# A recurrence's read-out on TensorE: one product per channel, or four channels as four 32-column tiles

## The reference

```python
r, k, v, w = ...                      # each (b, l, 32 heads, 8)
g = silu(xg @ Wg.T)
def step(s, rkvw):                    # s: (b, head, i, j), 8 x 8 per head
    a   = k_t[..., :, None] * v_t[..., None, :]
    out = einsum('bhi,bhij->bhj', r_t, u * a + s)
    s   = a + w_t[..., :, None] * s
    return s, out
# per head of 8 outputs: subtract the mean, divide by the deviation
og = normalized(out) * gn_w + gn_b
x1 = x + og * g @ Wo.T                # then the feed-forward part
```

## Time and profile before

| what | value |
|---|---|
| median of three executions | 2283.3 us (2282.72 to 2286.55) |
| span of the profiled execution, first to last instruction | 2282.6 us |
| its own time beside the span | not recorded; the median stands 0.7 us above the span |
| mean granted TensorE clock | 0.950 |
| TensorE busy | 1881.2 us, 82% |
| VectorE busy | 1497.5 us, 66% |
| ScalarE busy | 883.1 us, 39% |
| GpSimd busy | 879.3 us, 39% |

### The profile page before, as it was taken

How to read it: one execution, slowest core, us unless ns; L and a number is a source line. 1 busy time by engine, 2 the same in 40 slices (tenths; PEclk the granted TensorE clock), 3 DMA queues, 4 the chain that set the end, 5 groups by cost and what they waited for, 6 DMA issues and landing times. The chain is left out here.

```text
span 2282.6 us, 31354 instructions
## 1 busy us (share of the span) xinstructions
PE 1881.2 (82%) x10673; PEld 1165.9 (51%) x10673; DVE 1497.5 (66%) x2416; ACT 883.1 (39%) x1696; POOL 879.3 (39%) x928
## 2 busy tenths in 40 slices
PE   3888887889878897888978889788887899788765
PEld 2565444654447544564446644465445654356423
DVE  4654579736886369764697547973589746876274
ACT  1434442534425334254333543244432543425202
POOL 4522256312762137421373215631256313752060
PEclk9999999999999999999999999999998999999967
DMA  5000011010210102000020101201011010200030
GB/s 152 1 1 22 6 34 43 1 37 1 47 29 1 37 1 61 15 27 11 15 61 1 31 8 29 47 1 32 7 42 34 1 36 1 61 15 10 2 75 9
DMA packets 69291, 59.79 MB, mean 26 GB/s; under 512 B 34664, under 2 KB 52216, under 8 KB 69112
## 3 DMA queue, kind: packets, MB, share of 16 engines
q1 hardware_dynamic: 49592, 41.70, 8.2%
q10 hardware_dynamic: 18976, 15.80, 2.3%
q0 software_dynamic: 544, 0.03, 0.0%
HBM read 19.23 MB, written 4.19 MB: 10 GB/s over the span
## 5 line engine op out<-in xcount | busy, mean ns | idle before, releaser
L1498 POOL TENSOR_TENSOR soft_ring<-soft_ring,seg_max 128x512 f32<-128x512 f32 x256 | 326.9, 1277 | 586.1 <-DVE seg_max L1337 585.5
L1044 ACT ACTIVATE soft_ring<-soft_ring 128x512 f32<-128x512 f32 x256 | 161.1, 629 | 580.6 <-POOL soft_ring L1498 577.4
L1460 POOL TENSOR_TENSOR late<-late 128x520 f32<-128x520 f32 x128 | 212.4, 1659 | 64.4 <-DMA late<-late 49.7
L1331 DVE SCALAR_TENSOR_TENSOR soft_ring<-bank,mask 128x512 f32<-128x512 f32 x256 | 174.7, 683 | 94.7 <-PE bank L839 44.4
L660 PE MATMUL bank<-late,pick 128*128 128x512 f32 x256 | 162.2, 721 | 76.9 <-DVE late L1185 76.9
L583 PE MATMUL bank<-early 128*128 128x512 f32 x384 | 201.9, 611 | 18.4 <-ACTq L1037 13.6
L1173 DVE TENSOR_TENSOR_SCAN late<-late 128x520 f32<-128x520 f32 x128 | 204.2, 1595 | 18.3 <-POOL late L1462 11.0
L1337 DVE TENSOR_REDUCE seg_max<-soft_ring 128x8 f32<-128x512 f32 (+1 forms) x256 | 174.9, 683 | 26.8 <-DVE early L1352 9.5
L846 PEld LDWEIGHTS bank<-ident,soft_ring 128*128 128x128 f32 x1024 | 130.3, 148 | 80.5 <-issue 69.1
L839 PEld LDWEIGHTS bank<-early,qring 128*128 128x128 f32 x1024 | 138.4, 203 | 64.4 <-issue 61.7
L846 PE MATMUL bank<-ident,soft_ring 128*128 128x128 f32 x1024 | 164.0, 285 | 0.5 <-ACT soft_ring L1044 0.2
(11 more groups left out here) (242 smaller groups left out, 3456.1 us busy)
## 6 DMA issues: line engine op xcount, KB each, us to landing
late<-late SPq DMA_DIRECT2D x128, 260.0 KB, 3.0
c<-in_ctx ACTq DMA_DIRECT2D x8, 512.0 KB, 3.8
x<-in_x ACTq DMA_DIRECT2D x8, 512.0 KB, 6.5
out_x<-late SPq DMA_DIRECT2D x8, 512.0 KB, 6.4
w<-in_L_xattn_mlp_w ACTq DMA_DIRECT2D x2, 1024.0 KB
mask<-in_mask_BxS_ik SPq DMA_DIRECT2D x8, 256.0 KB, 3.7
mask<-in_mask_Bx1xSxS_ff ACTq DMA_DIRECT2D x8, 128.0 KB, 3.8
wkv<-in_L_xattn_kv_w ACTq DMA_DIRECT2D x1, 512.0 KB
```

The lines of the kernel that those rows point to most:

```text
L1044: af(soft[:, u % SOFT, :], soft[:, u % SOFT, :], ACT.Exp).then_inc(sig("exp"), 1)
L1331: stt(out=cuts(u, soft[:, u % SOFT, :]), in0=cuts(u, t[:, :]), scalar=HD1 ** -0.5 if u < UNITS else 1.0 / HD2, in1=mask.unsqueeze(1).broad ...
L1460: tt(aj[:, n % 2, :], kP[:, k, :, :].rearrange("p b t -> p (b t)"), vj[:, n % 3, :], ALU.mult).then_inc(sig("kv_done"), 1)
L1498: tt(s, s, seg_max[:, u % SOFT, 0:segs].unsqueeze(2).broadcast_to([128, segs, 512 // segs]), ALU.subtract).then_inc(sig("sub"), 1)
```

## The change

Output channels are collected four at a time. The `rs` ring has four buffers. In every fourth scan stage TensorE issues four products, each with a stationary of 128 x 32 columns, into PSUM partitions 0 to 31, 32 to 63, 64 to 95 and 96 to 127. Column 16*e + head of the stationary sums that head for the channels 4*e to 4*e + 3 (e = 0, 1); the two collections of a half accumulate. So head outputs come out ordered by channel: partition 32*(j % 4) + 16*(j // 4) + head. What meets them has to be in that order too: the rows of Wv and Wg, the columns of Wo, the head scales gn_w and gn_b, the matrices for centering, variance and bonus. They are permuted once in the setup: VectorE copies the rows and Wo in the new order before TensorE transposes them, and Wv and Wg on the way out of PSUM. The read of `vj` is now from 16 adjacent partitions. GpSimd's memset of `pick`, whose line is not in the diff, covers the new, smaller tensor (64 elements a partition instead of 1024).

```diff
+RS = 4
-        pick = sb("pick", [128, HS, 128])
+        pick = sb("pick", [128, 2, 2, 16])
-        rs = cut(late, 8808, 2, 512)
+        rs = cut(late, 8808, RS, 512)
+        def by_lane(ap):
+            return ap.rearrange("p (h e c) -> p c e h", e=2, c=4)
+        def lane(j):
+            return 32 * (j % 4) + 16 * (j // 4)
@@ setup, TensorE
-                nc.tensor.transpose(t[:, 0:128], vrows, ident[:, :]).then_inc(full, 1)
+                nc.tensor.transpose(t[:, 0:128], vrows, ident[:, :])
+                pe.wait_ge(sig("lane_rows"), 1)
+                nc.tensor.transpose(t[:, 128:256], vrows_by_lane, ident[:, :]).then_inc(full, 1)
+                    if w == "Wo":
+                        pe.wait_ge(sig("lane_wo"), 1)
+                        src = wo_by_lane
@@ setup, VectorE
-                for j in range(HS):
-                    nc.vector.tensor_copy(pick[:, j, :].rearrange("p (h j) -> p h j", j=HS)[:, :, j], block8[:, :, j])
+                (heads8, same8, pick and center8 built from block8 and ident: a memset, five copies, a reduction, the old center8 operation)
+                dve.wait_ge(sig("rows_all"), 1)
+                dve.wait_ge(sig("more_rows_in"), 16 * (15 + 2))
+                nc.vector.tensor_copy(vrows_by_lane.rearrange("p (c e h) -> p c e h", c=4, e=2), by_lane(vrows)).then_inc(sig("lane_rows"), 1)
+                dve.wait_ge(sig("square_in"), 16 * len(SQUARE))
+                for o in range(KT):
+                    for m in range(KT):
+                        at = slice(128 * m, 128 * m + 128)
+                        ins = nc.vector.tensor_copy(wo_by_lane[:, o, at].rearrange("p (c e h) -> p c e h", c=4, e=2),
+                                                    by_lane(cut(early, 512 * SQUARE.index("Wo"), KT, E)[:, o, at]))
+                ins.then_inc(sig("lane_wo"), 1)
                 normalize_ahead(dve, link)
...
+                    if w in ("Wv", "Wg"):
+                        (four copies of 128 x 128 through by_lane instead of one of 128 x 512)
@@ SyncE
-                            sp.dma_start(vj[:, n % 3, :], vP[j::HS, k, :, :]...
+                            sp.dma_start(vj[:, n % 3, :], vP[lane(j):lane(j) + 16, k, :, :]...
@@ TensorE, scan stages
-                            if 0 <= n < KT * HS:
+                            if 0 <= n < KT * HS and n % 4 == 3:
                                 pe.wait_ge(sig("rs_ready"), n + 1)
-                                mm(t[:, :], pick[:, j, :], rs[:, j % 2, :], start=j == 0, stop=j == HS - 1).then_inc(
-                                    full if j == HS - 1 else sig("rs_used"), 1)
+                                for c in range(4):
+                                    ins = mm(t[32 * c:32 * c + 32, :], pick[:, e, :, :], rs[:, (n - 3 + c) % RS, :], start=e == 0, stop=e == 1)
+                                ins.then_inc(full if e == 1 else sig("rs_used"), 1)
@@ VectorE, read(n)
-                            if n >= 2:
-                                m = n - 2
-                                if m % HS == HS - 1:
-                                    filled(("o3", m // HS))
+                            if n >= RS:
+                                quad = (n - RS) // 4
+                                if quad % 2 == 1:
+                                    filled(("o3", quad // 2))
                                 else:
-                                    dve.wait_ge(sig("rs_used"), m - m // HS + 1)
+                                    dve.wait_ge(sig("rs_used"), quad // 2 + 1)
```

More of the change, by code:

```diff
@@ L167, in build @@
         nmax0 = sb("nmax0", [128, 2 * NP, 2])
-        late = sb("late", [128, 10856])
+        late = sb("late", [128, 9832 + 512 * RS])
         x3 = sb("x3", [128, NP, E])
@@ L195, in build @@
         vrows = early[:, 8192:8320]
+        vrows_by_lane = early[:, 8320:8448]
+        wo_by_lane = cut(early, 8448, KT, E)
         soft = soft_ring[:, :, :]
@@ L445, in _ @@
                 nc.vector.tensor_copy(ones2[:, 0:16], half[:, :, :].rearrange("p a b -> p (a b)"))
-                link(nc.vector.scalar_tensor_tensor(out=center8[:, :], in0=flat8, scalar=-1.0 / HS, in1=ident[:, :], op0=ALU.mult, op1=ALU.add))
-                for j in range(HS):
-                    nc.vector.tensor_copy(pick[:, j, :].rearrange("p (h j) -> p h j", j=HS)[:, :, j], block8[:, :, j])
+                nc.vector.memset(pick[:, :, :, :], 0.0)
+                nc.vector.tensor_copy(heads8[:, :, :], block8[:, :, 0].unsqueeze(1).broadcast_to([128, 8, 16]))
+                link(nc.vector.tensor_reduce(same8[:, 0, :], ident[:, :].rearrange("p (a h) -> p h a", h=16), X, ALU.add))
+                for e in range(2):
+                    nc.vector.tensor_copy(pick[:, e, e, :], block8[:, :, 0])
+                link(nc.vector.tensor_copy(same8[:, 1:8, :], same8[:, 0, :].unsqueeze(1).broadcast_to([128, 7, 16])))
+                link(nc.vector.scalar_tensor_tensor(out=center8[:, :], in0=same8[:, :, :].rearrange("p a h -> p (a h)"), scalar=-1.0 / HS,
+                                                    in1=ident[:, :], op0=ALU.mult, op1=ALU.add))
+                dve.wait_ge(sig("rows_all"), 1)
[8 more added lines that the diff above has]
+                ins.then_inc(sig("lane_wo"), 1)
                 normalize_ahead(dve, link)
@@ L466, in _ @@
                     t, free = take(dve, w)
-                    nc.vector.tensor_copy(wt[w][:, :, :].rearrange("p k n -> p (k n)"), t[:, :]).then_inc(free, 1)
+                    if w in ("Wv", "Wg"):
+                        for k in range(KT):
+                            for m in range(KT):
+                                at = 256 * k + 128 * m
+                                ins = nc.vector.tensor_copy(wt[w][:, k, 128 * m:128 * m + 128].rearrange("p (c e h) -> p c e h", c=4, e=2),
+                                                            by_lane(t[:, at:at + 128]))
+                        ins.then_inc(free, 1)
+                    else:
+                        nc.vector.tensor_copy(wt[w][:, :, :].rearrange("p k n -> p (k n)"), t[:, :]).then_inc(free, 1)
                 dve.wait_ge(sig("plain_all"), 1)
@@ L668, in layer3 @@
                                 pe.wait_ge(sig("sq_ready"), k + 1)
-                                product((stage, k), 512, [(block8[:, :, :], sq[:, k, :])], "late")
+                                product((stage, k), 512, [(same8[:, :, :], sq[:, k, :])], "late")
                         elif stage == "project":
```

20 lines of the change are left out of this document (11 added, 9 removed).

## The result

The kernel after takes 2316.4 us (median of 4 runs, 2315.2 to 2317.4), the one before 2283.0 in the same session (4 runs, 2281.3 to 2286.6): ratio 1.0143, 95% interval 1.0131 to 1.0155. It is 33 us slower; the forecast was 2287 with a range to 2300. First the page of after: its span is 2313.9, 31.3 above that of before.

What follows compares the result with a forecast made beforehand. The prediction held that VectorE, with GpSimd tied to it through the scans, sets the scan stage's pace. Setup +7.1, stage -5.6 and tail +1.8 gave +3.3 us on a span of 2282.6: forecast 2287, range 2275 to 2300.

Steps and rivals of the forecast that it cites:

- removed work: Scan stage: twelve of 16 product slots a group go; the one ahead of values2 is won, 0.9 us a group.
- Rival (a): TensorE's clock stays low longer over L786 and what follows: 1.5 us a group lost, 2297 us; chance 28%.
- The new wait: Scan stage: reads wait for a quad issued one stage later; scan 10's idle 1.33 us covers it: 0, else up to 1 us a group.
- Setup: VectorE's moments and normalization move behind the wait for the rows, lengthening its chain: +7.1 us, bounds 5.5 and 9.5.
- Rival (d): The longer setup chain is hidden, as when ScalarE's loads end the setup anyway: 2279.5 us; chance 8%.
- The four tiles: Scan stage: four tiles run together, a quad taking 1.1 us, so 0.1 us a group more at the last quad.
- Rival (c): The tiles run serially, a quad taking 3.4 us warm and 6.8 cold: 2322 us; chance 4%.
- Transfers: Broadcast vj reads from 16 adjacent partitions take about twice as long but stay hidden: 0, at most 4.4 us once.
- Tail: After the last group: low-clock quads between reads, a later last quad and slower centering products: +1.8 us, bounds 0 and 4.
- Rival (b): TensorE binds more than the waits say, so all 2.7 us a group are won: 2274 us; chance 15%.

Runs made afterwards that it cites:

- e4: The kernel before with twelve of sixteen read-out products a group cut to 8 columns, nothing else of the change: 2297.7 us.
- e1: The changed kernel with an all-zero 128x512 product in each of the 12 emptied scan stages of a group: 2296.9 us.
- e8: The changed kernel with all-zero products only in the emptied stages of channels 4, 5 and 6 of each half: 2296.7 us.
- e12: The changed kernel with setup normalization before lane copies, quads one stage earlier, interleaved value rows, and zero products for channels 4, 5, 6 of each half: 2276.1 us.
- e13: As e12 without the all-zero products: the changed kernel with normalization before lane copies, quads one stage earlier and interleaved value rows: 2289.8 us.
- e3: The changed kernel with the setup's normalization ahead of the lane copies and their waits in VectorE's program: 2310.2 us.
- e10: The changed kernel with 32-column products issued singly, one a scan stage, and setup normalization before the lane copies, no zero products: 2290.9 us.
- e5: The kernel before with only the value read changed, to 16 adjacent partitions (sums other channels, same sizes): 2286.7 us.
- e9: As e7 with interleaved value rows, a channel on every second partition of 32: 2276.4 us.
- e11: As e10 with interleaved value rows, a channel on every second partition of 32: 2287.3 us.
- e2: The changed kernel with each quad issued one scan stage earlier in TensorE's program: 2298.3 us.
- e14: The kernel before with value rows read from every second partition (sums other channels, same sizes): 2283.5 us.
- e6: The changed kernel with all-zero products in all twelve emptied stages of a group and setup normalization before the lane copies: 2291.7 us.
- e7: As e6 with the quads issued one scan stage earlier as well: 2285.9 us.

## Why the prediction was wrong

The step that failed is the stage's "removed work": "the granted clock rises within 366 to 367 us, about as early with L786 moved up against the transposes", and with it that the slot at 363.06 is won. It names two things that the rows did not allow. L786 could not move up: its PSUM bank was not free, and the product n=6 ahead of it hid that. An engine that works through a wait shows no wait, and the earlier trace rows printed no releaser at 365.73 for that reason. And the clock did not rise as early, because it was that product which kept TensorE working up to L786. The forecast had -0.9 us a group for the removed work, and -0.8 for the whole stage; the group became 3.8 us longer (26.7 by 7). What was to be won is there in small: the wait of the copy (L1454, L1412 before) on the values went from 1.1 to 0.5 us, behind a read that now waits 4 us. VectorE's waits on TensorE, 329.2 to 420 us (total, times, longest), against the earlier trace rows:

```profile
DVE late L1227 <- PE bank L702: 4.0, 1, 4.0
DVE early L1448 <- PE bank L828: 3.4, 1, 3.4
...
DVE early L1454 <- PE bank L841: 0.5, 1, 0.5
```

**Rival (a)** was the mechanism, in its own words: "The product between kept TensorE without a gap; without it there are gaps." I gave it 28% and 2297. Its price of 1.5 us a group counted one L786 at the low clock. There are two query products a group, 1.3 and 1.8 us longer (3.75 for 2.49, and 3.78 for 1.99 in six of seven groups), and the first has the quad and the read queued behind it. e4 shows the clock's part alone; e1, e8, and e12 against e13, show it given back. The Trainium skill (TensorE: Matmul & The Clock Gate, Part 1, What's actually happening) puts it as "the default state is throttled, and activity releases the throttle"; the trace agrees, with 0.50 after the idle pause and 1.00 after a stretch without one.

**The new wait.** "Cost 0; with that cover gone, up to 1 us a group" was mis-sized with the same error. I put the quad at 367.3 to 368.4, before its read; it stood at 371.99, 3.68 after the start of the query product. The read waits 3.98 us, the idle 1.33 of the scan covers a part, and 1.4 us a group are left at the first head addition (59.9 for 58.5). The order of the argument was right (the cover, and its price if gone), but I gave "cover gone" the price of the old schedule.

**Setup.** Right: +7.0 for +7.1, and by the chain named. The rows of after:

```profile
31.53 0.28 DVE L473 COPY early<-early 128x128 f32<-128x128 f32 x1 [20.14 <-SPq L383]
...
36.51 1.38 DVE L304 TENSOR_SCALAR early<-c,mv,rstd 128x256 f32<-128x256 f32 x4 [0.67 <-ACT rstd L287]
...
49.39 0.42 DVE L523 TENSOR_TENSOR row_b<-row_b,late 128x256 f32<-128x256 f32 x1
```

VectorE is idle 20.14 us ahead of work that was ready before, then does the moments and, at 36.51, the normalization, inside the chain. Rival (d) falls; e3 confirms with 6.3 us.

**The four tiles.** Right in that they run together: 1.07 us at the full clock, one product's time. Rival (c) falls. But the next matmul starts 0.99 us after the quad, and not 0.86 as after a product.

```profile
347.81 1.07 PE L702 MATMUL bank<-late,pick 128*32 128x512 f32 x8 [1.66 <-DVE late L1227]
348.80 0.70 PE L624 MATMUL bank<-early 128*128 128x512 f32 x1
```

By the Trainium skill (TensorEngine Tiling (Array Packing), Key Properties) a change of the tiling mode drains TensorE. The trace agrees: the change there and back costs 0.33 us (4.35 for 4.02 us, with e10 above), in a wait of VectorE, where the forecast had 0.1 us a group. The overlap that I read as "no drain of note" does not speak against it: matmul records overlap everywhere, and only the distances of their starts show the price. The estimate of 2.2 us for seven groups met the measured 2.3, by luck: its 0.16 us was not the price of a change of tiling.

**Transfers.** Cost 0 was wrong. The landing went from 3.0 to 4.4 us, less than the doubling that I had allowed for, and still it was not hidden. At the tail's start the pipeline fills faster than the steady 2.8 us a step that I took as cover: in the kernel before GpSimd's second product starts 1.5 us after its first,

```profile
2187.11 1.28 POOL L1460 TENSOR_TENSOR late<-late 128x520 f32<-128x520 f32 x1 [49.69 <-DMA late<-late]
...
2188.61 1.28 POOL L1460 TENSOR_TENSOR late<-late 128x520 f32<-128x520 f32 x1
```

and in e5 2.4 us after, having waited 0.84. The bound that I gave, 4.4 us once at the tail's start, holds e5's 3.3. The Trainium skill (SBUF — State Buffer, Door 1: The DMA port swizzle) agrees with all three layouts: by its table every second partition of 32 reaches 8 ports, as every eighth does, and they land alike at 3.0; 16 adjacent ones reach 4, at 4.4.

**Tail.** +2.0 for +1.8, by luck and by another cause: the first part of the tail is 35.5 in before, 37.4 in after, 37.3 in e5 with the transfers alone, and 35.5 again in e9, e11 and e12. The quads run at the low clock, in 1.93 us where I had put 2.1 to 2.4, and are hidden; the centering costs nothing (47.2 for 47.3).

**Rival (b)** is refuted in the strong form. e4 frees TensorE of the same work and is slower. There was a slot to be won, but another one than I counted: the 0.86 us behind the second query product, which early quads take out of VectorE's wait for the scores.

What stays open: interleaving gave 9.5 us where quads were early and fillers in, 3.6 with single tiles, about 2.2 from e2 to e13 (8.5, of which the setup's order is 6.3), and e14 shows no gain from the layout in the old schedule. The tail accounts for 3.6 of the 9.5 (54.5 to 51.8 in its two parts, 48.2 to 47.3 behind them). The profiled execution of e9 took 2283.0, the longest of its six, so its trace does not show the rest. Nor is it shown why the last two groups are some 4 us longer in after. The sixth has it in e1, e6, e8, e10 and e11 as well (its third part is some 175 us where before has 173), and not in e7 and e9.

## What to carry to other kernels

Before counting a removed TensorE instruction as won, ask what TensorE will do in its place. If it will be idle ahead of a product that another engine waits for, the instruction was paying for the clock, and may have hidden a wait that no row prints. A cheap test is the old kernel with the candidate work shortened in place (e4): one kernel, and it would have shown the sign here. When a collection of several results replaces single ones, the collection belongs ahead of the next long product in TensorE's queue, not behind it; and small tiles among whole products pay for each change. And where a permuted layout is free to choose, spread over a stretch of partitions the rows that one transfer reads.

## What the runs showed of the hardware

- Forty-eight products of zeros, added on TensorE, made the kernel 13.7 us faster (e13 to e12, 2289.8 to 2276.1). The idle time ahead of the quad and the first query product of a group, which they fill, is 1.7 us.
- Eight records of 32 columns on four tiles take 1.07 us, two of a 128-column product 1.02; at the low clock 1.93 to 1.94 and 1.92. A quad or a single tile between whole products costs 0.33 us more than a whole product in its place (4.35 and 4.33 us for 4.02).
- Issued one by one, the tiles keep TensorE busy as long as full products: 160.7 us in e10 where before has 162.2.
- A broadcast read from 16 adjacent partitions lands in 4.4 us, from every second or every eighth in 3.0; the queue's share of the DMA engines' time goes from 8.2% to 13.3% and back to 8.4%. Spreading by two is enough.
